# ReLU attention with a periodic FFN on one core: score banks emptied as an early and a late pair by both engines, value product two steps behind

## The reference

```python
x = x + attn(layernorm(x));  x = x + ffn(layernorm(x))
# attn: 16 heads of 8 features
w    = relu(q @ k.T / sqrt(8));  w = w / (w.sum(-1) + 1e-6)
y    = x_in + (w @ v) @ w_out + b_out          # x_in: attn's own input
attn = layernorm(y) * gamma + beta
# ffn
sqrt((x @ cos(theta + theta_noise))**2 + (x @ sin(phi + phi_noise))**2)
```

## Time and profile before

| | before |
|---|---|
| median of the runs | 468.88 us |
| their range | 467.94 to 469.19 us |
| span of the profiled execution (first to last instruction) | 465.5 us |
| median less that span | 3.4 us |
| PE busy | 452.7 us, 97% |
| DVE busy | 366.3 us, 79% |
| ACT busy | 298.0 us, 64% |
| granted TensorE clock, mean | 1.000 |

### The profile page before, as it was taken

How to read it: one execution, slowest core, us unless ns; L and a number is a source line. 1 busy time by engine, 2 the same in 40 slices (tenths; PEclk the granted TensorE clock), 3 DMA queues, 4 the chain that set the end, 5 groups by cost and what they waited for, 6 DMA issues and landing times.

```text
span 465.5 us, 8651 instructions
## 1 busy us (share of the span) xinstructions
PE 452.7 (97%) x3374; PEld 151.2 (32%) x3374; DVE 366.3 (79%) x509; ACT 298.0 (64%) x339; POOL 41.1 (9%) x52
## 2 busy tenths in 40 slices
PE   6899999999999999999999999999999999999995
PEld 5533323222233232323233233233223233323234
DVE  5676889777878977878788977878787986888857
ACT  2666666677665667666665567666666567666643
POOL 3991000000000001000000001000000001100001
PEclk9999999999999999999999999999999999999999
DMA  5217810000000000100000000100000000000000
GB/s 152 70 45 148 175 40 25 1 23 1 2 24 1 24 0 12 37 1 25 0 23 0 23 0 0 45 0 23 0 23 0 0 0 0 23 0 0 0 1 23
DMA packets 6997, 11.50 MB, mean 25 GB/s; under 512 B 1760, under 2 KB 3168, under 8 KB 6592
## 3 DMA queue, kind: packets, MB, share of 16 engines
q1 hardware_dynamic: 6912, 11.08, 9.8%
q0 software_dynamic: 64, 0.13, 0.1%
HBM read 1.77 MB, written 1.05 MB: 6 GB/s over the span
## 4 chain that ended last, share of the span: by engine, by line
PE 92%; DVE 3%; ACT 2%; DMA 1%; SPq 1%; issue 0%; DVEq 0%
PE pv L857 56%; PE sc L827 28%; PE pv L864 3%; PE pv L905 1%; ACT w_buf L444 1%; DMA x_sb<-x_dram 1%; PE pv L878 1%; PE pv L772 1%; PE pv L762 1%; DMA q_rep<-q_lo 1%; SPq L267 0%; PE pv L756 0%; DVE x L661 0%; DVE inv_var L542 0%; PE sc L864 0%
## 5 line engine op out<-in xcount | busy, mean ns | idle before, releaser
L577 DVE TENSOR_SCALAR w_buf<-sc 128x1024 f32<-128x1024 f32 x256 | 312.8, 1224 | 83.5 <-PE sc L827 80.0
L444 ACT ACTIVATE w_buf<-sc 128x1024 f32<-128x1024 f32 x256 | 262.0, 1024 | 142.3 <-PE sc L827 141.6
L857 PE MATMUL pv<-w_buf,v_sb 128*32 128x512 f32 x2048 | 283.1, 605 | 0.0
L827 PE MATMUL sc<-q_rep,k_rep 32*128 32x512 f32 x1024 | 151.1, 495 | 2.2 <-DMA q_rep<-q_lo 1.2
L827 PEld LDWEIGHTS sc<-q_rep,k_rep 32*128 32x128 f32 x1024 | 69.2, 181 | 216.9 <-issue 179.3
L857 PEld LDWEIGHTS pv<-w_buf,v_sb 128*32 128x32 f32 x2048 | 43.1, 108 | 71.9 <-issue 59.3
L379 POOL TENSOR_TENSOR x<-x,mv 128x512 f32<-128x512 f32 (+1 forms) x5 | 4.4, 885 | 333.9 <-DVE x L661 333.9
L780 PE MATMUL pv<-ident 128*128 128x128 f32 x76 | 11.6, 323 | 1.5 <-POOL ident L327 1.5
L780 PEld LDWEIGHTS pv<-ident 128*128 128x128 f32 x76 | 11.2, 236 | 2.0 <-POOL ident L327 1.5
L864 PE MATMUL pv<-ident,pv_sb 128*128 128x128 f32 x60 | 9.8, 287 | 0.0
L389 POOL TENSOR_TENSOR mag<-sq 128x256 f32<-128x256 f32 x6 | 4.4, 729 | 57.8 <-ACT sq L478 57.8
(11 more groups left out here) (98 smaller groups left out, 138.0 us busy)
## 6 DMA issues: line engine op xcount, KB each, us to landing
q_rep<-q_lo SPq DMA_DIRECT2D x32, 64.0 KB, 2.1
q_rep<-q_hi SPq DMA_DIRECT2D x30, 64.0 KB, 2.1
k_rep<-k_hi SPq DMA_DIRECT2D x6, 256.0 KB, 4.1
k_rep<-k_lo SPq DMA_DIRECT2D x6, 256.0 KB, 5.5
x_sb<-x_dram SPq DMA_DIRECT2D x4, 256.0 KB, 4.1
out_dram<-x SPq DMA_DIRECT2D x3, 256.0 KB, 2.5
k_rep<-k_hi SPq DMA_DIRECT2D x8, 64.0 KB, 2.0
k_rep<-k_lo SPq DMA_DIRECT2D x8, 64.0 KB, 2.1
```

Of the source, the lines that this page charges most:

```text
L444: nc.scalar.activation(w_buf[:, s % W_STEPS, 0:2, :], sc[2 * s % PSUM_PAIRS][:, :, :], ACT.Relu).then_inc(relu[0], 1)
L577: nc.vector.tensor_scalar(w_buf[:, s % W_STEPS, 2:4, :], sc[(2 * s + 1) % PSUM_PAIRS][:, :, :], 0.0, None, ALU.max).then_inc(relu[1], 1)
L827: last = nc.tensor.matmul(sc[buf][:, i % 2, :], k_rep[rows, g, k * P:(k + 1) * P], q_rep[rows, g, :], start=True, stop=True)
L857: last = nc.tensor.matmul(bank[32 * i:32 * i + 32, :], v_sb[:, k, HPG * g + i, :], w_buf[:, s % W_STEPS, i, :], start=(k == 0), stop=(k == ...
```

## The change

Each score bank is emptied by an instruction of its own. Of a step's early pair (heads 0 and 1) ScalarE takes head 0 and VectorE head 1. Of its late pair (heads 2 and 3) ScalarE takes head 2 and VectorE head 3, but in the steps listed in `BOTH_LATE_ACT` (20 of the 64 of a pass: key tiles 3, 8, 9, 10, 11, 13, 14 of group 0; 1, 3, 8, 12, 15 of group 1; 3, 7, 11, 15 of groups 2 and 3) ScalarE takes both with one instruction and VectorE none. Both `relu` semaphores count pairs now, two a step, and each score pair and each value step waits for both. The value product of a step is issued two steps later (`LAG`), its heads in the order 0 to 3, after both waits. From pair 72 on (`TURN`, the early pair of step 36) the buffers of a pass shift by one, so that the ring of three also closes from one pass to the next.

```diff
+LAG = 2
+BOTH_LATE_ACT = ((3, 8, 9, 10, 11, 13, 14), (1, 3, 8, 12, 15), (3, 7, 11, 15), (3, 7, 11, 15))
+TURN = 2 * (2 * NT + 4)
...
+        def pair_bank(pair):
+            return (pair if pair < TURN else pair + 1) % PSUM_PAIRS
+        def freed_by(pair):
+            before = [p for p in range(pair) if pair_bank(p) == pair_bank(pair)]
+            if before:
+                return before[-1], 0
+            return [p for p in range(2 * STEPS) if pair_bank(p) == pair_bank(pair)][-1], 1
+        def act_takes_both(s):
+            return s % NT in BOTH_LATE_ACT[s // NT]
...
                 def relu_step(c, s):          # ScalarE
+                    early, late = sc[pair_bank(2 * s)], sc[pair_bank(2 * s + 1)]
                     act.wait_ge(scores[0], STEPS * c + s + 1)
-                    nc.scalar.activation(w_buf[:, s % W_STEPS, 0:2, :], sc[2 * s % PSUM_PAIRS][:, :, :],
+                    nc.scalar.activation(w_buf[:, s % W_STEPS, 0, :], early[:, 0, :], ACT.Relu).then_inc(relu[0], 1)
+                    act.wait_ge(scores[1], STEPS * c + s + 1)
+                    n = 2 if act_takes_both(s) else 1
+                    nc.scalar.activation(w_buf[:, s % W_STEPS, 2:2 + n, :], late[:, 0:n, :],
                                          ACT.Relu).then_inc(relu[0], 1)
...
                 def relu_step(c, s):          # VectorE
-                    dve.wait_ge(scores[1], STEPS * c + s + 1)
-                    nc.vector.tensor_scalar(w_buf[:, s % W_STEPS, 2:4, :], sc[(2 * s + 1) % PSUM_PAIRS][:, :, :],
-                                            0.0, None, ALU.max).then_inc(relu[1], 1)
+                    early, late = sc[pair_bank(2 * s)], sc[pair_bank(2 * s + 1)]
+                    dve.wait_ge(scores[0], STEPS * c + s + 1)
+                    nc.vector.tensor_scalar(w_buf[:, s % W_STEPS, 1, :], early[:, 1, :],
+                                            0.0, None, ALU.max).then_inc(relu[1], 2 if act_takes_both(s) else 1)
+                    if not act_takes_both(s):
+                        dve.wait_ge(scores[1], STEPS * c + s + 1)
+                        nc.vector.tensor_scalar(w_buf[:, s % W_STEPS, 3, :], late[:, 1, :],
+                                                0.0, None, ALU.max).then_inc(relu[1], 1)
...
+                        user, back = freed_by(pair)
                         if not (first and back):
-                            pe.wait_ge(relu[user % 2], STEPS * (c - back) + user // 2 + 1)
+                            pe.wait_ge(relu[0], 2 * STEPS * (c - back) + user + 1)
+                            pe.wait_ge(relu[1], 2 * STEPS * (c - back) + user + 1)
...
-                    for i in (1, 2, 3, 0):
-                        if i in (1, 2):
-                            pe.wait_ge(relu[i // 2], STEPS * c + s + 1)
+                    pe.wait_ge(relu[0], 2 * STEPS * c + 2 * (s + 1))
+                    pe.wait_ge(relu[1], 2 * STEPS * c + 2 * (s + 1))
+                    for i in range(HPG):
...
                     for s in range(STEPS):
                         score_step(c, s)
-                        if s == 0:
-                            if isinstance(c, int) and c == 0:
+                        if s < LAG:
+                            if not (isinstance(c, int) and c == 0):
+                                value_step(c - 1, STEPS - LAG + s)
+                            elif s == 0:
                                 project_v(1)
                                 transpose_x(2)
-                            else:
-                                value_step(c - 1, STEPS - 1)
-                            continue
+                            if s == 0:
+                                continue
...
-                        value_step(c, s - 1)
+                        if s >= LAG:
+                            value_step(c, s - LAG)
```

More of the change, by code:

```diff
@@ L809, in score_step @@
                         pair = 2 * s + half
-                        buf = pair % PSUM_PAIRS
-                        if pair >= PSUM_PAIRS:
-                            user, back = pair - PSUM_PAIRS, 0
-                        else:
-                            user, back = next(p for p in range(2 * STEPS - 1, 0, -1) if p % PSUM_PAIRS == buf), 1
+                        buf = pair_bank(pair)
+                        user, back = freed_by(pair)
                         if not (first and back):
-                            pe.wait_ge(relu[user % 2], STEPS * (c - back) + user // 2 + 1)
+                            pe.wait_ge(relu[0], 2 * STEPS * (c - back) + user + 1)
+                            pe.wait_ge(relu[1], 2 * STEPS * (c - back) + user + 1)
                         elif buf == 0:
@@ L941, in _ @@
                     run_pass(c, after_pass(c - 1))
-                value_step(NC - 1, STEPS - 1)
+                for s in range(STEPS - LAG, STEPS):
+                    value_step(NC - 1, s)
                 halves = [Part(NC - 1, 0), Part(NC - 1, 1)]
```

## The result

The changed kernel takes 454.19 us, the median of four runs (452.41 to 455.53), against 468.77 before; the ratio is 0.9687, 95% interval 0.9664 to 0.9711. I had forecast 445.4, range 439 to 454. The direction was right, the gain of 23.5 us was 14.6.

A forecast was written before the change was run, and what follows sets the result against it. It took PE's waits for the second score pair's buffer as the bound; waiting would fall from 33.5 to 3.8 + 4.7 + 1.5 = 10.0 us, the span from 465.5 to 442.0, plus 3.4 giving 445.4 us, range 439 to 454.

The forecast's parts named there:

- What bounds the kernel now: Score loads wait for the second pair's buffer; periods alternate 1.43 and 1.60, all waiting 33.5 us, about 21 of it alternation.
- One bank per instruction: VectorE clips 0.69 long, 0.60 start to start; the 0.19 wait becomes a margin of 0.1, ordinary step 1.43.
- Value product two steps behind: Value product needs a clip done a whole step ahead; moved pv hooks cost 0, head order 0, bound +-0.02 a step.
- More waits: PE's second waits per score pair and value group hide in its running ahead: 0, up to 0.1 a step without cover.
- Rivals 2 and 3: In each step, VectorE waits hold up PE's next work, 456 us (0.07); waits and issue fill the period, 477 us (0.05).
- rival 1: VectorE becomes the bound around the hooks, a bank costing 0.66 not 0.60: 5 to 7 us back, 451 us; chance 0.15.
- the signs of being wrong that I named: Ordinary periods above 1.45, or VectorE running without idle time over stretches with no hook.
- The hooks: Engines' work beside the clips makes them late: 1.25 us a pass in passes 1 to 3, 4.7 in pass 0, 1.5 unlisted.
- the 0.25 reckoned for tile 2 of group 1: ScalarE has both late banks and its pv copy at tile 1: 0.5 late, less 0.25 margin, leaves 0.25 of waiting.
- The sum: Waiting falls from 33.5 to 10.0 us, 23.5 less: span 465.5 to 442.0, median 445.4 us.
- The 3.4 us between span and median: The runs' median was taken to lie 3.4 above the profiled span, turning 442.0 into 445.4 us.

The follow-up runs named there:

- e10: Kernel before with TensorE's passes written out and only the value product moved to two steps behind, one clip an engine and step kept: 465.91 us, ratio 0.994.
- e1: Changed kernel with TensorE's passes 1 to 3 written out instead of looped, nothing else changed: 443.73 us, ratio 0.9473.
- e6: Changed kernel with passes written out and the BOTH_LATE_ACT list emptied, so VectorE takes one bank of every pair: 451.44 us, ratio 0.964.
- e5: Changed kernel with passes written out and the value product one step behind its scores instead of two: 455.58 us, ratio 0.9719.
- e2: Changed kernel, loop kept, without each value step's two waits that the score pairs' waits imply, except in a pass's last two steps: 450.24 us, ratio 0.9604.
- e3: Kernel before with four more always-met wait instructions a step in TensorE's loop, order of work unchanged: 477.15 us, ratio 1.0183.
- e9: e2's looped kernel with head 3 left out of the value product at key tiles 1 to 14 of passes 1 to 3: 442.64 us, ratio 0.9414.
- e8: Changed kernel with passes written out, e2's waits left out, and four more steps in which ScalarE takes both late banks: 443.13 us, ratio 0.9468.
- e4: Kernel before with TensorE's passes 1 to 3 written out: 468.05 us, ratio 0.9996.
- e7: Kernel before with two more always-met wait instructions a step, only before each score pair: 477.43 us, ratio 1.0198.

## Why the prediction was wrong

*What bounds the kernel now: right.* The release of a pair set the period. Periods of 1.43 and 1.60 stayed when only the distance changed (e10) and went when the pairs were emptied earlier as well (e1).

*One bank per instruction: right, sizes too.* 0.60 start to start, 0.69 long, margin enough, ordinary period 1.43. The estimate from the Trainium skill's table, "VectorE: DVE Perf Modes", TRN2 errata, was 0.66; rows of e6 show 0.60. The same section of the Trainium skill asks for 512 elements or more an instruction, and the new clips have 512, so it spoke less against the change than I had it. From the two sizes that I named, 1.13 for 1024 and 0.26 for 128, the upper end of the split is 0.63 and not 0.66; the 0.60 taken did not hang on it.

*Value product two steps behind: right.* With one step the values wait (e5).

*More waits: this step failed.* I wrote that the second waits of the score pairs and value groups hide in PE's running ahead, and took 0 for them. In the steps they do: 1.43 with and without the value waits (e1, e2). What I did not price is that a second wait is an instruction, some three a step and one more of register work, and that 250 more in the loop body move it past what stays fetched. Two jumps then cost 8.9 us in the profiled run; e3 prices them at 8.8 with nothing else changed, e1 and e9 take them away. The page of before had the sign: its queue 8 fetched 14 packets in all, the last one in the loop at 221 us, so passes 2 and 3 ran from code already there, and I did not ask how near the limit that was. I had looked for the cost of a wait in time alone, and the earlier trace rows answer only that. Rivals 2 and 3 looked in the same place, the step, and are refuted by its 1.43, as rival 1 is by the 0.60 of a bank. None of the signs of being wrong that I named appeared: I had named none outside the step and the hooks.

A warning was to be had. The Trainium skill, "Runtime: NRT & Kernel Launch", section on instruction fetch mechanics, says that code comes in pieces of 256 instructions, that PE has room for 2048, and that a taken branch whose target is not in the current window of two pieces waits for a fetch. The runs agree on the wait and its occasion. They agree with neither size as the limit of a loop: 1824, 1887, 1949 and 1950 instructions all stalled, 1663 and 1699, far more than two pieces, did not. By 2048 the changed loop would have fitted, by two pieces the loop before would have stalled too; the Trainium skill would have told me what to look at, not what would come.

*The hooks: right in sum.* Waiting left in e1: from its first scores at 17.85 to the end of its last values at 424.76 are 406.9, less PE's 398.4 = 8.5 us, against 10.0 forecast. A pass of 1 to 3 has 1.4 against 1.25: in group 0 periods of 1.66, 1.62 and 1.76 at tiles 11, 13 and 15, then 1.60 at tile 0 of group 1. The places differ in part: the 0.25 reckoned for tile 2 of group 1 is 0.02 there and 0.20 at tile 3, and `TURN` costs 0.08 at step 36 and not 0.2. Lateness after a hook of group 0 came about as reckoned; e8 showed that the late bank cannot cure it.

*The sum.* Without the jumps the forecast of 445.4 stands against e1's 443.73. Waiting was 1.5 less than forecast. The 3.4 us between span and median had a part of chance: a run takes about 1.8 us more than its own span (452.41 against 450.6, the others alike), and the rest came from a profiled execution with the clock at 1.000, where most runs of the same kernel in the record have 0.991 to 0.996; in e1 the difference is 3.0. Forecast and e3's 8.8 us together give 454.2, and that this meets the measured 454.19 is luck in part: from median to median the changed kernel lies 10.5 above e1, and the rest of the sum was 1.7 too high.

The profiled run's first scores started at 18.97 against 17.74 before, and this is not the change's. It goes with the clock granted from 7 to 17 us: 1.00 in before (17.74), 0.83 in e3, e4 and e1 (18.33, 18.36 and 17.85), 0.66 in after and e5 (18.97 and 19.00).

## What to carry to other kernels

Count what an edit adds to a loop body on each engine, not only what it costs in time; a second wait on an instruction is one more instruction. On the page, the packets of the instruction queue tell whether a loop runs from code already fetched; if they keep coming in every pass, look at the length of the branch, and write the loop out, which cost nothing here. An idle stretch put down to "issue" right at a loop's jump was a fetch of code here; the length of the branch tells.

When two engines empty what a third fills, let both work on the part that is wanted first: here the part that ended the wait came free earlier, and the wait of the ordinary step went.

## What the runs showed of the hardware

| kernel | instructions in TensorE's loop body | its branches, us | packets on queue 8 |
|---|---|---|---|
| e9 | 1663 | 0.24, 0.22 | 14 |
| before | 1699 | 0.24, 0.22 | 14 |
| e7 | 1824 | 3.33, 3.34 | 32 |
| e2 | 1887 | 3.89, 3.88 | 33 |
| after | 1949 | 3.85, 3.68 | 36 |
| e3 | 1950 | 3.34, 3.59 | 33 |

Where the branches are long, code is fetched throughout passes 2 and 3. Nothing between 1699 and 1824 was tried, and nothing shows whether the place at which a loop begins in the code moves the limit. A jump costs more than its branch: behind it PE ran into a second hole of about 1 us (230.4 to 230.8 and the group drawn out around it), and where the clock was granted at half level afterwards (332.5 to 335.0, after 2.83 us without a matmul) steps took up to 2.5 us. After the first jump's 2.94 us the clock stayed at full level. The changed kernel's runs spread over 3.1 us, from 452.41 at a mean granted clock of 0.986 to 455.53 at 0.976, those of e1 over 1.4, from 442.48 at 0.996 to 443.85 at 0.992.
